# Sixteen source-tile rows for the edge types: 132 message rounds of four or three gathers and eight fetches instead of 120 of four and eight

## What is computed

```python
m_in = jnp.concatenate([x[src], edge_emb_W[edge_type]], axis=-1)
m = jax.nn.relu(m_in @ msg_W.T + msg_b)
agg = jax.ops.segment_sum(m, dst, num_segments=N) / jnp.clip(deg, 1.0)[:, None]
h = x + agg @ upd_W.T + upd_b
out = layer_norm(h) * ln_g + ln_b
```

## Time and profile before

| what | us |
|---|---|
| median of 3 runs (range) | 5477.21 (5473.35 to 5478.56) |
| the profiled execution, time | 5464.72 |
| the profiled execution, span | 5463.0 |
| PE busy in the span | 3347.2 (61%) |
| DVE busy in the span | 4046.6 (74%) |
| ACT busy in the span | 1883.2 (34%) |
| POOL busy in the span | 3917.0 (72%) |

### The profile page before, as it was taken

How to read it: one execution, slowest core, us unless ns; L and a number is a source line. 1 busy time by engine, 2 the same in 40 slices (tenths; PEclk the granted TensorE clock), 3 DMA queues, 4 the chain that set the end, 5 groups by cost and what they waited for, 6 DMA issues and landing times.

```text
span 5463.0 us, 73672 instructions
## 1 busy us (share of the span) xinstructions
PE 3347.2 (61%) x22715; PEld 2079.5 (38%) x22716; DVE 4046.6 (74%) x6653; ACT 1883.2 (34%) x2463; POOL 3917.0 (72%) x2523
## 2 busy tenths in 40 slices
PE   1323222222222566777533477769999999899998
PEld 1322222222221222222333222225444445699997
DVE  5799988889884998999699899982612110677776
ACT  1000000000002446999544499980001110433334
POOL 0388888888888888999888789983056650477786
PEclk6555555555556878999755799999999999999999
DMA  9622222222226983343599534348775677344454
GB/s 408 216 1 1 1 1 1 1 1 1 1 1 190 352 321 99 102 109 93 153 318 316 179 102 109 93 101 283 255 266 193 223 239 258 110 145 148 145 146 110
DMA packets 507288, 790.25 MB, mean 145 GB/s; under 512 B 294189, under 2 KB 389788, under 8 KB 469400
## 3 DMA queue, kind: packets, MB, share of 16 engines
q1 hardware_dynamic: 336886, 750.71, 41.6%
q0 software_dynamic: 164128, 35.36, 9.2%
q10 hardware_dynamic: 6146, 2.68, 0.2%
HBM read 603.67 MB, written 165.59 MB: 141 GB/s over the span
## 4 chain that ended last, share of the span: by engine, by line
POOL 26%; PE 20%; DVE 18%; issue 17%; DMA 8%; ACT 3%; SPq 1%; DVEq 0%; POOLq 0%; ACTq 0%
PE PS L753 18%; POOL edge_weight_and_count L682 17%; POOL feature_major L741 10%; DVE tiles L1745 7%; DVE feature_major L1685 5%; DVE tiles L1738 4%; DMA tiles<-edge_weight_and_count 4%; DMA copies_then_records<-edge_count 3%; PE PS L930 1%; ACT copies_then_records L1292 1%; DVE smax L1697 0%; DMA edge_weight_turned<-copies_then_records 0%; PE PS L1113 0%; DMA edge_weight_turned<-turned_tail 0%; SPq L499 0%
## 5 line engine op out<-in xcount | busy, mean ns | idle before, releaser
L703 POOL DMA_INDIRECT sorted_edges<-record_slot,place_slot x784 | 1629.2, 2078 | 277.0 <-issue 230.3
L682 POOL DMA_INDIRECT edge_weight_and_count<-weight_and_count,target x784 | 1234.4, 1574 | 448.0 <-issue 245.6
L741 POOL DMA_INDIRECT feature_major<-message_table,copies_then_records x480 | 580.4, 1209 | 370.5 <-DMA message_table<-node_major 224.4
L797 PE MATMUL PS<-consts,key_slot 128*128 128x128 f32 x798 | 198.2, 427 | 1026.0 <-DVE target L1560 1022.4
L753 PE MATMUL PS<-tiles,node_major 128*128 128x448 f32 (+1 forms) x2100 | 817.5, 547 | 10.4 <-ACT node_major L1218 10.4
L753 PE MATMUL PS<-tiles 128*64 128x392 f32 (+1 forms) x3200 | 630.2, 515 | 282.8 <-DVE tiles L1745 280.0
L1745 DVE SCALAR_TENSOR_TENSOR tiles<-tiles,copies_then_records 128x1568 f32<-128x1568 f32 (+1 forms) x400 | 698.6, 1781 | 13.2 <-ACT tiles L1323 12.5
L1685 DVE SCALAR_TENSOR_TENSOR feature_major<-tiles,s,feature_major 128x1600 f32<-128x1600 f32 (+3 forms) x384 | 679.4, 1848 | 35.7 <-ACT tiles L1279 35.5
L722 POOL DMA_INDIRECT paired_edges<-copies_then_records,edges x328 | 327.3, 998 | 391.8 <-issue 349.1
L797 PEld LDWEIGHTS PS<-consts,key_slot 128*128 128x128 f32 x798 | 155.0, 223 | 1048.1 <-DVE target L1560 1044.3
L753 PEld LDWEIGHTS PS<-tiles,node_major 128*128 128x128 f32 (+1 forms) x2100 | 399.7, 193 | 387.9 <-issue 372.2
(11 more groups left out here) (362 smaller groups left out, 4996.2 us busy)
## 6 DMA issues: line engine op xcount, KB each, us to landing
tiles<-edge_weight_turned SPq DMA_DIRECT2D x72, 1568.0 KB, 8.2
tiles<-edge_count SPq DMA_DIRECT2D x72, 1568.0 KB, 8.2
tiles<-edge_weight_and_count SPq DMA_DIRECT2D x48, 1600.0 KB
edge_weight_and_count<-feature_major SPq DMA_DIRECT2D x48, 1568.0 KB, 39.4
copies_then_records<-edge_count SPq DMA_DIRECT2D x192, 392.0 KB
tiles<-edge_weight_and_count SPq DMA_DIRECT2D x48, 1536.0 KB, 8.9
feature_major<-types_and_sources SPq DMA_DIRECT2D x120, 512.0 KB, 4.4
edge_weight_turned<-copies_then_records SPq DMA_DIRECT2D x48, 768.0 KB, 4.8
```

Of the source, the lines that this page charges most:

```text
L682: nc.gpsimd.indirect_dma_start(out=edge_d, out_offset=bass.IndirectOffsetOnAxis(ap=idx[:, s, a:a + 1], axis=0), in_=pay[:, s, a, :], in_of ...
L703: nc.gpsimd.indirect_dma_start(out=rec_d, out_offset=bass.IndirectOffsetOnAxis(ap=place_slot[:, s, a:a + 1], axis=0), in_=rec_slot[:, s, a ...
L741: nc.gpsimd.indirect_dma_start(out=msg[i % GATHERED][:, a, :], out_offset=None, in_=table_d, in_offset=bass.IndirectOffsetOnAxis(ap=rec[:, ...
```

## The change

Source tiles now have 112 nodes (`SR`), and there are 28 of them (`ST`). The other 16 partitions of every tile of source rows hold the 16 type rows in f32. The one-hot of a fetched chunk gets its rows 0 to 111 by the source and its rows 112 to 127 by the type: SP loads the source numbers to 112 partitions and the type numbers to 16, and one compare with `row_id` (the lane, and the lane less 112 from 112 on) makes both. So the type terms and type one-hots of the fetched chunks are gone, and one f32 matmul per fetched chunk gives source and type together. More and smaller source tiles need more fetched chunk slots: 132 rounds with 8 fetched chunks are 1056 slots, while the rounds take four and three gathered chunks in turn, 462 in all, and 346 chunks are regrouped. In `make_hots` the compares for types and sources no longer form one run: the source compare is split in two halves, and lane compares stand between the three. The source rows live in `source_rows` (over `P0` and the front of `P1`) instead of `NM`, and the matmul offsets in `NM` instead of `P0`. The table is written by seven DMAs of 112 partitions, and one more DMA lays the type rows into the source tiles. The turning of types and sources has a sixth stage.

```diff
-ROUNDS = 120
+ROUNDS = 132
+GATHERS = (4, 3)
+SR = TP - TYPES
+ST = NP // SR
-NA, NB = GA * ROUNDS, GB2 * ROUNDS
+NA, NB = sum(GATHERS) * ROUNDS // 2, GB2 * ROUNDS
...
             def load_types(i):
-                sp.dma_start(type_rows[i % RING], turned_d[i * GA:(i + 1) * GA, :].rearrange("c p -> (c p)").unsqueeze(0)
-                             .to_broadcast([TYPE_ROWS, GA * TP])).then_inc(S(f"types_in{i % RING}"), 16)
-                sp.dma_start(pair_rows[i % RING], turned_d[NA:NA + 2 * NB, :].rearrange("(k c) p -> k c p", k=2)[:, i * GB2:(i + 1) * GB2, :].rearrange("k c p -> k (c p)").unsqueeze(0)
-                             .to_broadcast([TP, 2, GB2 * TP])).then_inc(S(f"types_in{i % RING}"), 16)
+                first, n = gathered_at(i), GATHERS[i % 2]
+                sp.dma_start(type_rows[i % RING][:, 0:n * TP], turned_d[first:first + n, :].rearrange("c p -> (c p)").unsqueeze(0)
+                             .to_broadcast([TYPE_ROWS, n * TP])).then_inc(S(f"types_in{i % RING}"), 16)
+                for rows_, first in ((slice(0, SR), NA + NB), (slice(SR, TP), NA)):
+                    sp.dma_start(pair_rows[i % RING][rows_], turned_d[first + i * GB2:first + (i + 1) * GB2, :].rearrange("c p -> (c p)").unsqueeze(0)
+                                 .to_broadcast([rows_.stop - rows_.start, GB2 * TP])).then_inc(S(f"types_in{i % RING}"), 16)
             sp.wait_ge(S("h3_ready"), 1)
+            sp.dma_start(source_rows[SR:TP, :, :], type_part[0:TYPES, :].unsqueeze(1).to_broadcast([TYPES, ST, D])).then_inc(S("types_out"), 16)
...
-                for a in range(GA):
+                for a in range(GATHERS[i % 2]):
...
                 i = 4 * RANK_TILES.index(t) + b // 2
-                if b % 2 or b // 2 > 3 or i >= NT:
+                if b % 2 or b // 2 > 3 or i >= ST:
                     return
...
-                    if k == 5 and t in (4, 8, 12, 16, 20):
+                    if k == 5 and t in (4, 8, 12, 16, 20, 24):
                         turn_types(t // 4 - 1)
...
             def fill(u, half, at):
                 for c in range(GH):
-                    out_ap = SM[:, c * TP:(c + 1) * TP]
-                    type_term(out_ap, u, GA + half * GH + c, False)
-                    last = nc.tensor.matmul(out_ap, src_hot[u][:, half * GH + c, :], NMf[:, bass.ds(at[c], D)],
-                                            start=False, stop=True, skip_group_check=True)
+                    last = nc.tensor.matmul(SM[:, c * TP:(c + 1) * TP], src_hot[u][:, half * GH + c, :], source_flat[:, bass.ds(at[c], D)],
+                                            start=True, stop=True, skip_group_check=True)
                 last.then_inc(S("blocks_filled"), 1)
...
-                for b in range(PAIR):
-                    v.tensor_scalar(hot[u][:, b, :], lane_row[:, :], lane[:, i, b:b + 1], None, ALU.is_equal)
-                dve.wait_ge(S(f"types_in{u}"), 32 * (i // RING + 1))
-                v.tensor_scalar(type_hot[u][:, 0:GA, :].rearrange("p b n -> p (b n)"), type_rows[u], type_id, None, ALU.is_equal)
-                v.tensor_scalar(type_hot[u][:, GA:PAIR, :].rearrange("p b n -> p (b n)"), pair_rows[u][0:TYPE_ROWS, 0, :], type_id, None, ALU.is_equal)
-                v.tensor_scalar(src_hot[u].rearrange("p b n -> p (b n)"), pair_rows[u][:, 1, :], col("lane_id"), None,
-                                ALU.is_equal).then_inc(S("hots_made"), 1)
+                def lanes_hot(first, stop):
+                    for b in range(first, stop):
+                        last = v.tensor_scalar(hot[u][:, b, :], lane_row[:, :], lane[:, i, b:b + 1], None, ALU.is_equal)
+                    return last
+
+                def sources_hot(half):
+                    at = slice(half * GH * TP, (half + 1) * GH * TP)
+                    v.tensor_scalar(src_hot[u][:, half * GH:(half + 1) * GH, :].rearrange("p b n -> p (b n)"), pair_rows[u][:, at],
+                                    col("row_id"), None, ALU.is_equal)
+
+                n = GATHERS[i % 2]
+                lanes_hot(0, n)
+                dve.wait_ge(S(f"types_in{u}"), 48 * (i // RING + 1))
+                v.tensor_scalar(type_hot[u][:, 0:n, :].rearrange("p b n -> p (b n)"), type_rows[u][:, 0:n * TP], type_id, None, ALU.is_equal)
+                lanes_hot(GA, GA + 3)
+                sources_hot(0)
+                lanes_hot(GA + 3, GA + 6)
+                sources_hot(1)
+                lanes_hot(GA + 6, PAIR).then_inc(S("hots_made"), 1)
```

More of the change, by code:

```diff
@@ L847, in count_columns @@
                 pe.wait_ge(S("spare_inputs_made"), 1)
-                for i in range(NT):
-                    last = mm(SM[0:COPIES, 0:MC], marker(i), marks[i], i == 0, i == NT - 1)
+                for i in range(ST):
+                    last = mm(SM[0:COPIES, 0:MC], marker(i), marks[i], i == 0, i == ST - 1)
                 last.then_inc(S("spare_results_made"), 1)
@@ L1094, in _ @@
             pe.wait_ge(S("h3_ready"), 1)
-            for t in range(NT):
-                n = rows_of(t)
-                last = mm(bigT[0:n, t, :], H[:, t * TP:t * TP + n], asel)
-                if t % 4 == 3 or t == NT - 1:
+            for t in range(ST):
+                last = mm(bigT[0:SR, t, :], H[:, t * SR:(t + 1) * SR], asel)
+                if t % 4 == 3:
                     last.then_inc(S("msg_x"), 1)
@@ L1139, in message_round @@
                     pe.wait_ge(S("blocks_bent"), i * 3)
-                for c in range(GA):
-                    last = type_term(SM[:, c * TP:(c + 1) * TP], u, c, True)
+                for c in range(GATHERS[g % 2]):
+                    last = type_term(SM[:, c * TP:(c + 1) * TP], u, c)
                 last.then_inc(S("blocks_filled"), 1)
@@ L1149, in message_round @@
                     pe.wait_ge(S("messages_made"), i * 1)
-                    scatter(msg[g_before], before, 0, at[0:4])
+                    scatter(msg[g_before], before, 0, at[0:GATHERS[g_before % 2]])
                 pe.wait_ge(S("blocks_bent"), i * 3 + 2)
@@ L1163, in _ @@
             pe.wait_ge(S("messages_made"), ROUNDS)
-            scatter(msg[GATHERED - 1], RING - 1, 0, more[0:4]).then_inc(S("scattered"), 1)
+            scatter(msg[GATHERED - 1], RING - 1, 0, more[0:GATHERS[1]]).then_inc(S("scattered"), 1)
             product([(adel, P0)], [("update_centred", 1)], "upd_out", ("agg_scaled", 0))
@@ L1806, in column_tiles @@
                 o(v.tensor_copy(col("lane_id"), col("lane_id").bitcast(I32)))
+                o(v.tensor_scalar(col("row_id"), col("lane_id"), float(SR), -float(SR), ALU.is_ge, ALU.mult))
+                o(v.tensor_tensor(col("row_id"), col("row_id"), col("lane_id"), ALU.add))
                 o(v.tensor_scalar(col("junk_id"), col("lane_id"), float((NB - NA) * TP), None, ALU.add))
@@ L1961, in split_records @@
                 stage(1)
-                for ahead, records, n in ((0, rec[:, 0:NA, 1], GA), (GA, part[:, :, 1], GB2)):
-                    to = lane[:, :, ahead:ahead + n]
-                    o(v.tensor_scalar(to.bitcast(I32), records.rearrange("p (i j) -> p i j", j=n), TYPE_STEP - 1, None, ALU.bitwise_and))
+                pairs = rec[:, 0:NA, 1].rearrange("p (i j) -> p i j", j=sum(GATHERS))
+                lanes = lane.rearrange("p (i r) j -> p i r j", r=2)
+                for to, records in ((lanes[:, :, 0, 0:GATHERS[0]], pairs[:, :, 0:GATHERS[0]]),
+                                    (lanes[:, :, 1, 0:GATHERS[1]], pairs[:, :, GATHERS[0]:]),
+                                    (lane[:, :, GA:PAIR], part[:, :, 1].rearrange("p (i j) -> p i j", j=GB2))):
+                    o(v.tensor_scalar(to.bitcast(I32), records, TYPE_STEP - 1, None, ALU.bitwise_and))
                     o(v.tensor_copy(to, to.bitcast(I32)))
```

104 lines of the change are left out of this document (58 added, 46 removed).

## The result

| what | before | after |
|---|---|---|
| median of 6 runs each (range), us | 5471.19 (5460.55 to 5478.56) | 5495.96 (5492.53 to 5509.28) |
| profiled execution: time, span, us | 5464.72, 5463.0 | 5499.79, 5498.0 |
| first and last gather of the loop, us | 4702.5, 5428.0 | 4719.5, 5459.3 |

The ratio after to before is 1.0053, with an interval of 1.0042 to 1.0063: the changed kernel is 25 us slower, where 61 us less were forecast. Of the 35 us between the two profiled executions 17.0 lie ahead of the first gather, 14.3 between first and last gather, 3.7 behind. The chips of the experiments differ: four groups of runs out of five fell on chips where every kernel, the one before included, took 6 to 7% longer, with waits that the trace calls "remote", because it finds nothing in the kernel that ended them.

What follows compares the result with a forecast made beforehand. POOL was taken to bound the loop (726.5 us), PE a near second; POOL's gain of 70.5 us less 5.4, 2.7 and 1.3 ahead of the loop gave 61, so 5477.2 − 61 = 5416 us, range 5386 to 5458.

Steps and rivals of the forecast that it cites:

- The hold: Message loop, POOL: long DVE compares delay gathers; splitting them lowers this from 0.81 to 0.38 us a round.
- the fourth: Loop rival: types compare through last lane compare act as one long hold, 2.3 us a round, 5671 us; chance 0.02.
- The third: Loop rival, lockstep: each of three compares holds a gather every round, 1.31 us, 5538 us; slower from 0.85; chance 0.07.
- A mean gather above 1.25 us: Sign in the loop's gathers that would prove the split compares wrong; a mean near 1.11 us was expected.
- The new round of PE, 4.79 us: Loop, PE: weight-load starts sum to 5.64 us a round before, 4.79 without the fills' type terms, 632 us in all.
- Rival 1: Loop: PE is the bound if gathers are held under 0.2 us a round, giving 5392 us; chance 0.25.
- The scatter of gathered chunks: Loop, PE: stays at 0.95 us with three chunks instead of four, because the next fill waits for ACT's read.
- Ahead of the loop: Costs before the first gather: rank rounds 5.4, SP 2.7, masks and table tiles 1.3 us.
- Rank rounds: Ahead of the loop, DVE: 25 become 28, three more at 1.79 us each, costing 5.4 us.
- SP and the last table tile: Ahead of the loop: four more DMA issues and a whole seventh table DMA delay the first gather by 2.7 us.
- DVE's wait for SP's rows: Loop: comes 1.6 us earlier, but is covered by loads issued about two rounds, 10 us, ahead; no cost.
- The rule on the shared port: Loop: VectorE in a two-port mode shuts GpSimd out for whole instructions, so lane compares would join holds; counted against the change.

Runs made afterwards that it cites:

- both mended: Changed kernel with DVE waiting after each source-compare half and PE's address loads moved ahead of its waits: 5485.9 us, 1.0049 of the kernel before.
- with fixed addresses: Changed kernel with one gather a round and fixed matmul addresses instead of those PE loads into registers; output not computed: 4.78 us a round.

## Why the prediction was wrong

- *The hold, forecast at 0.38 us a round*, is the first step that failed. The formula took each compare for itself, L²/1.31, with the lane compares between them as gaps. They are none: behind a long compare they prolong it. By the prediction's own sum (mean less median) the hold is (600.2 − 462 x 0.989)/132 = 1.09 us. The rest of that sum holds: 3.5 gathers of 0.989 + 0.304 are 4.53, with 1.09 they make 5.62, x 132 = 741 us; the loop shows 740. Of the four rivals the fourth had the mechanism, at 2.3 us a round about twice too dear. The third was nearer in number, 1.31 us a round, but takes a hold for the compares' own time, and the same compares hold by 0.52 to 1.73 us by their order. Its bound of 0.85 us, above which the kernel is slower, leaves PE out: at 0.46, both mended, the kernel was still slower (1.0049). A mean gather above 1.25 us was named as what would refute the split, and 1.299 came.
- *The new round of PE, 4.79 us*, is the second. Its weight loads and waits were right: with fixed addresses the round is 4.78. What the sum left out, with no reason given, are the address loads into PE's registers. The timeline does not list them, and no gap gave them away, because the type terms covered them; only the view by source line has them. Removing the cover laid them bare, 0.61 us a round. This step alone would have undone the forecast: at 5.39 x 132 = 711 us the loop gains 15 us, and 11 to 13 are lost ahead of it (17.0 less the 3.8 of the attention stage, or 11.3). Rival 1, PE as the bound at 5392 us, was thus right in kind for a kernel without holds and wrong by 80 us in its price.
- *The scatter of gathered chunks*, 0.95 us in rounds of three too because the next fill waits for ACT, was right for the sum it stands in: with fixed addresses the fill's loads start 0.96 us after the scatter's (5205.01, 5205.97), 0.21 of it for ACT. With the address loads in place they start after 0.68 us (5201.90, 5202.58).
- *Ahead of the loop*, 9.4 us forecast. Rank rounds 5.4, measured 6.3, as at tile 24 they stand 2.10 us apart and not 1.79. SP and the last table tile 2.7 and part of 1.3, measured 2.2. The first gathers were 17.0 us apart in the first pair of executions and 11.3 in the second; the difference is from execution to execution.
- *DVE's wait for SP's rows*, costed at nothing: no wait of DVE for them is in the trace. *DVE* waits 117.9 us for gathers, as forecast. Both were right.
- *The rule on the shared port.* A caught gather is held for whole instructions, and where the add follows at once, through it. The Trainium skill, "SBUF — State Buffer", section "Who interferes with whom", says that the engine that issues first has the port for the whole instruction, and that a tensor_tensor with both inputs in SBUF contends with GpSimd's reads. For gathers that a series caught (3.66 and 3.73 us above) the trace agrees that GpSimd is shut out for whole instructions, but the holds also run on over the joints between them, and both gathers' rows begin 0.31 and 0.24 us ahead of the long compare; when within its row a gather needs the port, no row shows. For lane compares behind an add (1.01 us at 4935.53) it still disagrees.

**What stays open:** how much of the 25 us the holds make. That they make the changed loop long is read from POOL's sum (600.2 + 133.9 + 6.7 = 740.8 us, only 6.7 of it waits for PE); no run on an undisturbed chip took the holds away and nothing else. Open too: what the order alone is worth there (holds of 0.52 against 1.12, but an estimate of at most 0.20 us a round down to PE's 5.39, 26 us); why lane compares let a gather through behind an add or a wait and keep it out behind a longer compare; and why the kernel before gains by set-apart compares on long chips. Of the kernels timed on the undisturbed chip none was faster than the kernel before.

## What to carry to other kernels

If another engine is held up by long instructions, breaking them up shortens the hold only with true gaps between them; short instructions put in between join them, and the order (long ones last, just ahead of a wait) decides how much is held. Before an engine is credited with the time of the work taken off it, ask what ran beneath that work: its sequencer's register loads are missing from busy times and timeline, so look them up by their source line, and measure the engine's own pace with the other bound removed. Relief for the bound is worth at most its distance to the next one (here POOL's 6.05 to PE's 5.83 us a round), not what its own sum says.

## What the runs showed of the hardware

- GpSimd's indirect DMAs, 0.97 us in the mean where VectorE waits after each long compare, take up to 5.45 us in the changed kernel, and the same VectorE work costs them 0.52, 1.12 or 1.73 us a round by its order alone.
- A wait of VectorE for its own last instruction shortens such holds: 0.34 to 0.46 us a round with it in the changed kernel, none left in the kernel before.
- 20 addresses a round, which TensorE's sequencer loads into registers in three loads of 0.59 us (median), cost 0.61 us where nothing covers them. Beneath the type terms of the kernel before they show as 0.02 us (2.2 us of "issue" in 120 rounds, with one gather each).
